# A decoder layer whose prologue is written in another order, with the first two contexts read at once and the maxima's transfers placed between high and low query transfers

## What is computed

```python
def reference(x, ctx_4096, ...):
    x = x + _L0_attn_ref(_layernorm(x), wq, wk, wv, wo)
    x = x + _L0_xattn_ref(_layernorm(x), ctx_4096, Wq_d, W_qk, Wkv_d, Wv_u)
    x = x + _L0_ffn_ref(_layernorm(x), gate, kernel, bias, lora_A, lora_B, lora_A_shared, lora_B_shared)

def _L0_xattn_ref(Q, K, Wq_d, W_qk, Wkv_d, Wv_u):
    C_q = Q @ Wq_d                       # 64
    C_kv = K @ Wkv_d                     # latents, 32
    CqWqk = (C_q @ W_qk).reshape(b, n, H, LKV)
    scores = jnp.einsum('bnhl,bkl->bhnk', CqWqk, C_kv) / jnp.sqrt(LKV)
    attn = softmax(scores)
    V_up = (C_kv @ Wv_u).reshape(b, nkv, H, HD)
    return jnp.einsum('bhnk,bkhd->bnhd', attn, V_up).reshape(b, n, H * HD)

def _L0_ffn_ref(...):
    A_eff = jnp.einsum('bn,nri->bri', gate, lora_A)      # over 16 adapters
    B_eff = jnp.einsum('bn,nor->bor', gate, lora_B)
    ...
```

## Time and profile before

| | us |
|---|---|
| median of 3 runs (679.02 to 682.49) | 679.2 |
| profiled execution, device time | 681.57 |
| its span, first to last instruction | 679.6 |
| PE busy | 591.6 (87%) |
| DVE, POOL, ACT busy | 442.2, 424.9, 303.8 |
| prologue, up to the first maxima matmul | 64.7 |
| a body in the loop, for example 502.30 to 575.30 | 73.0, PE busy 69.09 (95%) |
| SP standing inside its issue of wqk, from 8.54 | 10.8 |
| a_eff and b_eff on their way to memory, from 42.98 | 12.4 |
| read in the first 21 us | 7.04 MB (335 GB/s mean, some 400 once begun) |

### The profile page before, as it was taken

How to read it: one execution, slowest core, us unless ns; L and a number is a source line. 1 busy time by engine, 2 the same in 40 slices (tenths; PEclk the granted TensorE clock), 3 DMA queues, 4 the chain that set the end, 5 groups by cost and what they waited for, 6 DMA issues and landing times.

```text
span 679.6 us, 12918 instructions
## 1 busy us (share of the span) xinstructions
PE 591.6 (87%) x3856; PEld 306.8 (45%) x3856; DVE 442.2 (65%) x717; ACT 303.8 (45%) x641; POOL 424.9 (63%) x394
## 2 busy tenths in 40 slices
PE   4863988699999999998999999999999899986965
PEld 4331644353544554464456354455446444433322
DVE  2711796378776887489658867588758966745451
ACT  1330144335644374346534564337444744563450
POOL 5002027558965886598776896488659877789300
PEclk9895889799999999999989999999999999997896
DMA  8567630353116510481018311661048101100000
GB/s 310 211 210 245 236 119 18 78 210 166 43 29 228 211 44 1 115 323 57 17 42 271 154 43 31 225 215 43 1 130 333 32 15 47 43 9 1 22 1 14
DMA packets 31410, 77.22 MB, mean 114 GB/s; under 512 B 11378, under 2 KB 25042, under 8 KB 28915
## 3 DMA queue, kind: packets, MB, share of 16 engines
q1 hardware_dynamic: 31186, 75.36, 33.1%
q10 hardware_dynamic: 160, 1.05, 0.4%
HBM read 58.66 MB, written 2.88 MB: 91 GB/s over the span
## 4 chain that ended last, share of the span: by engine, by line
PE 62%; DVE 12%; issue 7%; POOL 6%; ACT 5%; SPq 3%; DMA 3%; POOLq 0%; ACTq 0%; DVEq 0%
PE st_ps L649 11%; PE mx_ps L677 10%; PE pv_ps L664 9%; POOL acc L1096 5%; PE mi_ps L459 4%; PE mi_ps L466 4%; PE mi_ps L453 4%; PE mi_ps L512 4%; SPq L371 3%; PE mi_ps L631 2%; DVE mx_p L1020 2%; DVE sm L982 2%; PE mi_ps L537 2%; DMA b_eff<-acc 2%; PE mi_ps L635 2%
## 5 line engine op out<-in xcount | busy, mean ns | idle before, releaser
L1096 POOL TENSOR_TENSOR acc<-acc,p_ring 125x448 f32<-125x448 f32 x300 | 359.8, 1199 | 49.2 <-ACT p_ring L833 23.5
L1020 DVE TENSOR_REDUCE mx_p<-mx_ps 128x1 f32<-128x500 f32 x336 | 210.7, 669 | 101.7 <-PE mx_ps L677 100.6
L833 ACT ACTIVATE p_ring<-st_ps 125x448 f32<-125x448 f32 x384 | 189.7, 544 | 171.4 <-PE st_ps L649 164.4
L649 PE MATMUL st_ps<-q_st,c_st 98*125 98x448 f32 x384 | 155.3, 432 | 13.4 <-ACT p_ring L833 7.7
L677 PE MATMUL mx_ps<-c_st,q_st 96*128 96x500 f32 x336 | 139.4, 446 | 14.9 <-DMA q_st<-q_hl 11.2
L649 PEld LDWEIGHTS st_ps<-q_st,c_st 98*125 98x125 f32 x384 | 68.7, 191 | 117.1 <-ACT p_ring L833 88.2
L1104 POOL TENSOR_TENSOR rstd<-mv,eps_col 128x1 f32<-128x1 f32 x24 | 4.6, 192 | 153.2 <-DVE mv L894 153.2
L664 PE MATMUL pv_ps<-p_ring,c_nat 125*32 125x448 f32 x768 | 94.4, 564 | 1.0 <-ACT p_ring L833 0.9
L677 PEld LDWEIGHTS mx_ps<-c_st,q_st 96*128 96x128 f32 x336 | 63.2, 196 | 41.4 <-issue 20.6
L1096 POOL TENSOR_TENSOR acc<-p_ring 125x448 f32<-125x448 f32 x30 | 36.6, 1221 | 27.3 <-ACT p_ring L833 27.3
L466 PE MATMUL mi_ps<-ctx_sb,wkv_sb 128*32 128x375 f32 x512 | 48.1, 496 | 0.7 <-DVE p L943 0.7
(11 more groups left out here) (111 smaller groups left out, 671.0 us busy)
## 6 DMA issues: line engine op xcount, KB each, us to landing
ctx_sb<-in_ctx_t SPq DMA_DIRECT2D x16, 3000.0 KB, 11.1
c_st<-ct_hl SPq DMA_DIRECT2D x192, 46.9 KB, 2.0
q_st<-q_hl SPq DMA_DIRECT2D x96, 56.0 KB, 2.0
x_sb<-in_x SPq DMA_DIRECT2D x16, 112.0 KB
out_y<-x3n SPq DMA_DIRECT2D x16, 112.0 KB
wq_sb<-in_wq SPq DMA_DIRECT2D x2, 512.0 KB, 4.4
ctx_sb<-in_lora_a SPq DMA_DIRECT2D x1, 1024.0 KB, 6.8
ctx_sb<-in_lora_b SPq DMA_DIRECT2D x1, 1024.0 KB, 8.7
```

Of the source, the lines that this page charges most:

```text
L649: mm(st_ps[unit % STB][0:KC, 0:HALF], c_st[:, b % 4, t * KT + k * KC:t * KT + (k + 1) * KC], q_st[:, b // 2 % 2, b % 2, half * HALF:(half ...
L833: act.activation(p_ring[:, unit % PR, :], st_ps[unit % STB][0:KC, 0:HALF], ACT.Exp, scale=float(L) ** -0.5).then_inc(exp_done, 1)
L1020: ve.tensor_reduce(mx_p[:, p:p + 1], mx_ps[unit % MXB][:, 0:KP], AX.X, ALU.max).then_inc(red_done, 1)
L1096: po.tensor_tensor(dst, first, p_ring[:, unit % PR, :].rearrange("p (h s) -> p h s", s=S), ALU.add).then_inc(acc_done, 1)
```

## The change

The main parts, in the order of the program:

- x comes padded to 64 rows for each batch and is read in one transfer of 128 rows; the memset of x_sb is gone. wk is read before wq.
- ACT's first instruction is an exponential on a spare column, with the table load ahead of it. PE does eight matmuls on ident before T1.
- Context 0 is read before the adapters, whose raw weights now lie in kern_sb, ox and x3n; context 1 and x of pair 1 are read behind wo.
- POOL makes gkron, and makes the masks before the first power.
- Ah and A of batch 0 go ahead of the wait for S3 and use a bank of mx_ps. P0 and P1 stand before the adapter products, and these are dealt out in portions of 2, 1, 4 and 1.
- SM0 stands between S1 and S2 on DVE.
- The queries of pair 0 go out by `spread_first_q`, six transfers from SP and six from ACT; the adapters' results are written behind them, and the waits for eff_out are in body 0 (ACT before its first exponential, POOL behind its first power, SP at the end).
- In the bodies SP issues the 8 high query transfers at H, then the two of the maxima at MT, then the 4 low ones.

```diff
-        spare = ctx_sb[:, 1, :, :].rearrange("p c k -> p (c k)")
-        lora_raw = [spare[:, 0:2048], spare[:, 2048:4096]]
+        lora_raw = [kern_sb[:, :, :].rearrange("p c n -> p (c n)"),
+                    ox[:, :, :, :].rearrange("p h b s -> p (h b s)")[:, 0:1536], x3n[:, :]]
...
+        def spread_first_q(dma, part, dst, t):
+
+            dma(q_st[dst:dst + L, 0, :, t * 4 * S:(t + 1) * 4 * S].bitcast(F32),
+                q_hl[t * L:(t + 1) * L, part, :, :].bitcast(F32)).then_inc(q_in[0], 16)
...
-                for h in range(2):
-                    dma(x_sb[h * SLOT:h * SLOT + S, n % 2, :], x[pair_index(n), h]).then_inc(x_in[n % 2], 16)
+                dma(x_sb[:, n % 2, :], x[pair_index(n)].rearrange("b s d -> (b s) d")).then_inc(x_in[n % 2], 16)
...
-            sp.wait_ge(dve_c, due(dve_c, 1))
             load_x(0)
...
-            sp.wait_ge(lora_ps, due(lora_ps, 8))
-            load_ctx(1)
+            sp.wait_ge(qh_hi, due(qh_hi, 1))
+            for t in range(4):
+                spread_first_q(dma, 0, 0, t)
+            for t in range(2):
+                spread_first_q(dma, 0, L, t)
+
+            sp.wait_ge(lora_ps, due(lora_ps, 4))
             dma(kern_sb[:, :, :], kern.rearrange("(c p) n -> p c n", p=128)).then_inc(w_ffn, 16)
...
-            sp.wait_ge(eff_out, due(eff_out, 32))
-            spread_q(0)
...
                         elif name == "MT":
                             spread_m(n)
+                            if n % 2 and n + 1 < B:
+
+                                spread_q((n + 1) // 2, 1, (2 * L,))
...
                         elif name == "H":
-                            spread_q(n)
+                            spread_q(n, 0, (0, L))
...
+            pe.wait_ge(w_latent, due(w_latent, 16))
+            for name in ("Ah", "A"):
+                step(name, 0)
             pe.wait_ge(s1_sb, due(s1_sb, 4))
...
+            for name in ("CQ", "H"):
+                step(name, 0)
+
+            act.wait_ge(qh_hi, due(qh_hi, 1))
+            for t in range(2, 4):
+                spread_first_q(act.dma_start, 0, L, t)
+            act.wait_ge(qh_lo, due(qh_lo, 1))
+            for t in range(4):
+                spread_first_q(act.dma_start, 1, 2 * L, t)
             act.wait_ge(lora_sb, due(lora_sb, 8))
...
-            for name in ("S0", "S1", "S2", "S3"):
-                step(name, 0)
-            ve.wait_ge(raw_in, due(raw_in, 16 * 3))
-            ve.tensor_tensor(gkron[:, :, :], g8[:, :].unsqueeze(2).to_broadcast([128, PAIRS, 8]),
-                             e8[:, :].unsqueeze(1).to_broadcast([128, PAIRS, 8]), ALU.mult).then_inc(dve_c, 1)
-            for name in ("SM0", "SM1", "SN0", "SN1", "AS"):
+            for name in ("S0", "S1", "SM0", "S2", "S3", "SM1", "SN0", "SN1", "AS"):
                 step(name, 0)
```

More of the change, by code:

```diff
@@ L194, in decoder_layer @@
         minus_half = sb("minus_half", [128, 1])
+        table = sb("table", [128, 1])
         eps_col = sb("eps_col", [128, 1])
@@ L842, in out_of_sums @@
                      pv_ps[:, 0:HALF].rearrange("p (h s) -> p h s", h=8)).then_inc(ox_sb, 1)
-            act.wait_ge(dve_c, due(dve_c, 2))
+            act.wait_ge(dve_c, due(dve_c, 1))
+            act.activation(table[:, :], minus_half[:, :], ACT.Exp)
             def lora_out(since, until):
```

105 lines of the change are left out of this document (65 added, 40 removed).

## The result

| | before | after |
|---|---|---|
| median of 4 runs each, us | 680.5 (679.0 to 682.5) | 691.7 (688.5 to 693.2) |
| span of the profiled execution | 679.6 | 686.4 |
| mean granted clock | 0.947 | 0.943 |
| prologue, up to the first maxima | 64.7 | 53.6 |
| bodies 0 to 6 | 510.9 | 528.7 |

A forecast was written before the change was run, and what follows sets the result against it. TensorE, busy 87% of the span, was taken as the loop's floor, so time could come only from where it stands. Prologue -13.0 and boundaries +6.2 give -6.8: from 679.2 to 672.4 us, range 665.5 to 679.5.

The forecast's parts named there:

- K starts: Prologue, start of the first projection: at 8.2 us against 10.66, once wv has landed; 2.5 us gained.
- K and Q: Prologue, the first projection and the queries' one together: 6.7 us.
- end of the softmax: Prologue, end of the softmax's second half: at 28.7 us against 31.42, 2.7 gained so far.
- O1: Prologue, PE's step after the transposes of P: starts at 32.9 us against 38.74, 5.8 gained so far.
- T2: Prologue, the second transpose: at 42.1 us against 48.65, 6.6 gained so far.
- high part ready: Prologue, high part of the first queries: ready at 46.3 us against 54.06, 7.8 gained so far.
- first maxima: End of the prologue, first maxima matmul: at 51.7 us against 64.66, 13.0 gained in all.
- seven boundaries: Where one body gives way to the next: new waits for the low query transfers, 6.2 us lost in sum.
- bodies otherwise: Bodies apart from their boundaries: nothing gained or lost, 0 us.
- Slower: Rival: new waits also bring the granted clock down at the six other boundaries, 12 us more, 684.4; chance 0.08.
- The boundaries lose nothing: Rival: other stalls swallow the boundaries' waits or low transfers land sooner; -13.0 alone, 666.2 us; chance 0.17.
- Half a prologue: Rival: the prologue gives only half, -6.5 with +6.2 at the boundaries, 678.9 us, no change; chance 0.15.

The follow-up runs named there:

- e17: The changed kernel with the hardware loop over bodies 2 to 5 instead of 1 to 6: 677.8 us, ratio 0.9969.
- e14: The changed kernel with its nine bodies written out, no hardware loop: 675.4 us, ratio 0.9947.
- e13: The changed kernel with the old order of transfers in the bodies and all nine bodies written out, no hardware loop: 670.5 us, ratio 0.9891.
- e18: e13 run once more, unchanged, for a narrower interval: 667.4 us, ratio 0.9823.
- e10: The changed kernel with two memsets of an unused column added to DVE's prologue: 684.7 us, ratio 1.0066.
- e2: The kernel before with only the four low query transfers moved behind the maxima's two: 694.9 us, ratio 1.0231.
- e8: e1 with two memsets of an unused column added to DVE's prologue: 677.3 us, ratio 0.9961.
- e1: The changed kernel with all 12 query transfers ahead of the maxima's again in the bodies: 680.3 us, ratio 1.0013.
- e16: e8 with the hardware loop over bodies 2 to 5 instead of 1 to 6: 667.8 us, ratio 0.9812.
- e15: e8 with six adapter products again ahead of the transposes of P and all twelve first query transfers on SP: 693.8 us, ratio 1.022.

## Why the prediction was wrong

| step | predicted | measured | |
|---|---|---|---|
| K starts | 8.2 | 9.49 | wv took 6.7 to land, not 5.4, beside more reads |
| K and Q | 6.7 | 7.3 | granted clock 0.50 up to 14.8 |
| end of the softmax | 28.7 | 30.2 | |
| O1 | 32.9 | 34.5 | 1.6 late, 1.3 of it from K |
| T2 | 42.1 | 43.7 | |
| high part ready | 46.3 | 47.8 | |
| first maxima | 51.7 | 53.6 | 5.8 after the high part, 5.4 foreseen |
| seven boundaries | +6.2 | +10.2 (waits for q_st 11.9, less 1.7 saved at m_t) | late landings behind bodies 2 and 4; body 0 |
| bodies otherwise | 0 | +7.6 (17.8 less 10.2) | clock: PE busy +5.7; exponentials +3.6; other waits less |

**The prologue** was right in mechanism at every step and 2 us too good in size. The failing term is K's: the landing of wv was taken from a row with less traffic beside it, and K and Q were priced as they ran before (6.7), but took 7.3, with the granted clock at 0.50 up to 14.8. The eight matmuls on ident did not speed K up: it took 2.07 us, as before. All that follows kept the distances that were foreseen within some 0.4 us, the two queues too.

**The boundaries** had the right mechanism and the right place. The term was mis-sized by one assumption in it, "+ 2.0" for the landing. It holds at five of the seven boundaries, where the low ones end at 5.9 to 6.0 after the copy, as against 5.8 foreseen. Where the loop's code starts again it was 3.3 and 3.1, and e17 moved it. The trace before held this already: behind body 2 its last query transfer took

```profile
q_st<-q_hl SPq DMA_DIRECT2D x1, 56.0 KB, 3.4
```

and 3.1 behind body 4. The prediction saw only that the maxima matmul started late there, took that as room, and so made these two its cheapest boundaries (0.6 and 0.3), where 2.6 and 2.3 were measured. Behind body 0 the wait was 2.5 where 1.2 was foreseen, and stays 2.2 without a loop (e14). I had put the low transfers' end 5.8 after m_t's copy, and here it is 5.9 (117.56 to 123.45), so what failed is the time that they were compared with. PE got its first score 1.1 earlier, at 120.39, and the row now calls the rest a wait for q_st; against the kernel before, that boundary costs 0.5. With no loop the order costs 4.9 by these medians (e14 against e13), or 8 by e18's: the +6.2 of the sum lies between.

**What was in no term** is the second large part, and it was taken at nothing without a row being named for it. One piece is the two instructions fewer on DVE ahead of the loop. They turn a tie between DVE and POOL, which the trace before already held (165.76 against 165.80), and cost 7.0 (e10). The other is the clock: the sum kept every body's matmuls at their old length, and PE was busy for 5.7 us longer over bodies 0 to 6. The two overlap, for a part of the half clock comes behind the waits that DVE's delay makes.

**The rivals.** "Slower" was right in sign, and its mechanism, the granted clock, is real in bodies 1, 3 and 5. But it named the six boundaries with their new waits as the cause, and of the six only the one behind body 2 has half clock behind it (from 281.1). In bodies 1 and 5 it begins 1.6 and 2.1 us behind the waits that DVE's subtraction makes. "The boundaries lose nothing" is refuted by e2. "Half a prologue" was wrong about the prologue itself, but right that a gain there is not simply passed on: e8 starts its loop 12.9 earlier than the kernel before and keeps 2.5. My sentence "whatever ends the prologue earlier moves everything behind it by as much" nearly holds without the loop (e13 keeps 10.3 of 11.6 by the profiles) and failed with it.

**The sum, by runs.** With the subtraction in its place, the new prologue gives -2.4 (679.7 to 677.3), the order of transfers +7.4 (677.3 to 684.7), and the place of DVE's code +7.0 (684.7 to 691.7). Together it is +12.0, against the measured +11.1. The shares depend on the way taken: the order costs 11.4 with DVE's code as it is in the changed kernel (e1), and 15.4 with the old prologue (e2).

**Open.** Why an earlier prologue meets longer restarts than the kernel before did: its wait for m_t behind body 2 was 0.2 where e8's was 2.8, and it too had a late landing there. In e8 six of SP's query issues took 5.16 us, 0.86 each, just ahead; when instruction packets come against when SP issues may decide it, but no run holds one fixed. Nor is it shown why DVE's instruction is 0.29 late at one place of its code and not at another.

## What to carry to other kernels

Don't put a short transfer that one instruction needs ahead of longer ones that the next instruction needs: the wait moves one instruction on and grows by the issues in between. If a kernel reuses code by a hardware loop, measure the body in which the code starts again apart from the others, and try fewer restarts, before the order of anything is tuned: here one restart instead of two was worth 9 us (e16 against e8) and 7 (e17 against e10). When a landing time goes into a sum, look it up at every place of the trace before where it is used, and not at one. And when a change that should be neutral isn't, look for two engines that start within 0.1 us of each other in the trace before.

## What the runs showed of the hardware

- The last of a series of 56 KB query transfers lands 2.0 us after its issue at most boundaries, and 2.8 to 4.0 in most cases where the hardware loop starts its code again, in whichever body that is (3.3 and 3.1 in the changed kernel, 3.6 behind body 3 in e17; the least are 2.4 in e8 and 2.2 in e15). All 82 landings of query transfers over 2.8 us (from 150 to 600 us of the 17 traces) had an instruction packet of queue 8 beside them, with and without a loop.
- DVE's subtraction over 128x896 takes 1.09 us alone, and 1.50 to 1.99 if POOL's addition starts before it and still runs. POOL's addition takes 1.13 alone, and 2.06 if DVE is first.
- Two DVE instructions more ahead of a loop made the whole 3.1 and 7.0 us shorter, without any change of work.
- A wait of 1.5 us on PE in the middle of a body had half clock behind it within 2.5 us in 8 of 12 places, a wait of 0.5 us in the same places of three kernels (nine places) in none.
- One issue of a 56 KB transfer on SP takes 0.64 us; twelve of them took 0.95 each while two transfers of 512 KB left for memory (e15).
- Eight matmuls on ident ahead of T1, taken at nothing in the sum, went with a T1 of 0.66 us instead of 1.09.
